# Last feed-forward stage of a two-layer gated cross-attention kernel: four PSUM banks for the down products instead of two, two of them shared with the up products

## The reference

```python
def _L1_ffn_ref(x, W_exp, b_exp, up_weights, up_bias, down_weights, W_con, b_con, down_bias):
    h = jnp.einsum('bsd,dh->bsh', x, W_exp) + b_exp
    h = butterfly(h, up_weights, D_HIDDEN)
    h = jax.nn.gelu(h + up_bias, approximate=False)
    h = butterfly(h, down_weights, D_HIDDEN)
    y = jnp.einsum('bsh,hd->bsd', h, W_con) + b_con
    return y + down_bias
...
x = x + jnp.tanh(g_ffn[1]) * _L1_ffn_ref(_layernorm(x, axis=-1), ...)
```

## Time and profile before

| | |
|---|---|
| runs of the kernel, us | 1150.83, 1146.01, 1144.23; median 1146.01 |
| the profiled execution, us | 1144.74, its span in the profile 1142.9 |
| busy over the span | PE 988.4 us, PEld 866.0, DVE 792.9, ACT 626.3, POOL 235.4 |
| the last stage | from about 943 us to the end of the span |
| slots 0 to 5 | about 25 us each |
| granted TensorE clock, mean | 0.926 of full speed |

### The profile page before, as it was taken

One profiled execution on the slowest core, in us unless ns is written; L12 is line 12 of the kernel. 1 busy time (PEld: TensorE's weight loads), 2 busy tenths in 40 slices (PEclk: granted clock), 3 DMA queues, 4 the chain that ended last, 5 costly groups with the idle time before them and its releaser, 6 DMA issues. The chain is left out here.

```text
span 1142.9 us, 20586 instructions
## 1 busy us (share of the span) xinstructions
PE 988.4 (86%) x6833; PEld 866.0 (76%) x6833; DVE 792.9 (69%) x1588; ACT 626.3 (55%) x1088; POOL 235.4 (21%) x424
## 2 busy tenths in 40 slices
PE   6489999998659998925699994999999989999998
PEld 5367767776448876725588994899999977888888
DVE  5357888875338989979959843677777768656672
ACT  4156666665357779968838543565656544222230
POOL 4213333220129300000002302122111104111210
PEclk9799999999759999967689996999999998999999
DMA  6745554445042237768712366655556610000001
GB/s 197 218 111 138 136 119 124 127 118 173 1 159 111 111 100 241 257 249 306 282 45 91 124 227 162 162 121 118 118 127 127 128 47 1 19 19 31 25 19 38
DMA packets 102808, 143.60 MB, mean 126 GB/s; under 512 B 42951, under 2 KB 76743, under 8 KB 100439
## 3 DMA queue, kind: packets, MB, share of 16 engines
q1 hardware_dynamic: 102438, 141.67, 43.1%
q0 software_dynamic: 304, 1.10, 0.3%
HBM read 76.30 MB, written 47.13 MB: 108 GB/s over the span
## 5 line engine op out<-in xcount | busy, mean ns | idle before, releaser
L41 PE MATMUL bank<-f_xt_hi,f_w_hi 128*128 128x512 f32 x320 | 130.5, 408 | 11.1 <-DMA f_xt_lo<-x_spill 7.9
L42 PE MATMUL bank<-f_xt_lo,f_w_hi 128*128 128x512 f32 x320 | 127.4, 398 | 0.0
L43 PE MATMUL bank<-f_xt_hi,f_w_lo 128*128 128x512 f32 x320 | 127.3, 398 | 0.0
L2631 ACT ACTIVATE f_h<-bank,f_b 128x512 f32<-128x512 f32 x64 | 43.4, 690 | 121.8 <-PE bank L43 74.0
L595 ACT ACTIVATE a_prob<-bank 77x512 f32<-77x512 f32 x128 | 72.5, 591 | 31.5 <-PE bank L759 31.0
L661 DVE TENSOR_REDUCE a_maxima<-bank 128x4 f32<-128x308 f32 x128 | 60.4, 472 | 41.4 <-PE bank L734 41.1
L41 PEld LDWEIGHTS bank<-f_xt_hi,f_w_hi 128*128 128x128 f32 x320 | 61.8, 193 | 27.0 <-DMA f_xt_lo<-x_spill 9.9
L41 PE MATMUL bank<-f_w_hi,f_h_hi 128*128 128x256 f32 x256 | 72.6, 284 | 8.1 <-DVE xres L2596 8.1
L756 PE MATMUL bank<-a_stack,a_kb 96*77 96x256 f32 x256 | 70.8, 299 | 4.7 <-ACT a_mt L588 4.7
L43 PE MATMUL bank<-f_w_hi,f_h_lo 128*128 128x256 f32 x256 | 72.2, 282 | 0.0
L42 PE MATMUL bank<-f_w_lo,f_h_hi 128*128 128x256 f32 x256 | 72.2, 282 | 0.0
(11 more groups left out here) (317 smaller groups left out, 3077.3 us busy)
## 6 DMA issues: line engine op xcount, KB each, us to landing
u_spill<-f_ubuf SPq DMA_DIRECT2D x48, 256.0 KB, 2.5
f_uback<-u_spill SPq DMA_DIRECT2D x24, 512.0 KB, 5.5
a_stack<-a_queries SPq DMA_DIRECT2D x16, 512.0 KB, 4.8
a_q_max<-a_q_hi SPq DMA_DIRECT2D x32, 256.0 KB, 4.9
a_kb<-a_key_spill SPq DMA_DIRECT2D x96, 77.0 KB, 2.5
f_mats<-in_low_steps SPq DMA_DIRECT2D x12, 512.0 KB, 6.6
xres<-in_x SPq DMA_DIRECT2D x16, 256.0 KB, 4.4
a_queries<-a_q_hi SPq DMA_DIRECT2D x16, 256.0 KB, 2.6
```

The source lines that it names most:

```text
L41: nc.tensor.matmul(out, w_hi, m_hi, start=start, stop=False)
L42: nc.tensor.matmul(out, w_hi, m_lo, start=False, stop=False)
L43: return nc.tensor.matmul(out, w_lo, m_hi, start=False, stop=stop)
L2631: act.activation(h[:, n % 2, :], hbank[n % 4][:, :], ACT.Gelu, bias=b1[:, n:n + 1]).then_inc(h_ready, 1)
```

## The change

The four down products of a group get a bank each. y(g, 0) and y(g, 1) stay in O0 and O1; y(g, 2) and y(g, 3) go into `hbank[2]` and `hbank[3]`, which in each slot are free between the up products of tile 6 and 7 of group g + 1 and those of tile 2 and 3 of group g + 2. The waits of PE follow: y(g, 0) and y(g, 1) wait for the sums of the same tiles of the group before, y(g, 2) and y(g, 3) for ACT's gelu of tile 6 and 7 of group g + 1, and h(g, 2) and h(g, 3) from g = 2 on for DVE's sums of tile 2 and 3 of group g - 2. In the last group each down product waits for the sum before it in its bank as well. Nothing is computed differently and no other step moves.

```diff
-        ybank = [O0, O1]
+        ybank = [O0, O1, hbank[2], hbank[3]]
...
-                    dve.scalar_tensor_tensor(out=x, in0=ybank[n % 2][:, 0:D], scalar=tg[:, 0:1], in1=x,
+                    dve.scalar_tensor_tensor(out=x, in0=ybank[n][:, 0:D], scalar=tg[:, 0:1], in1=x,
                                              op0=ALU.mult, op1=ALU.add).then_inc(y_added, 1)
...
                     if n == 0:
                         pe.wait_ge(xt_split, (g + 1) * DC)
-                    if not (isinstance(g, int) and g == 0 and n < 4):
+                    if n in (2, 3) and not (isinstance(g, int) and g < 2):
+
+                        pe.wait_ge(y_added, g * GTT + n - 3 - GTT)
+                    elif not (isinstance(g, int) and g == 0 and n < 4):
                         pe.wait_ge(h_ready, g * HT + n - 3)
...
                     if n == 0:
                         pe.wait_ge(h_split, (g + 1) * HT)
-                    if not (isinstance(g, int) and g == 0 and n < 2):
-                        pe.wait_ge(y_added, g * GTT + n - 1)
+                    if n >= 2:
+                        last_h = min(g + 2, G) if isinstance(g, int) else g + 2
+                        pe.wait_ge(h_ready, last_h * HT + n - 3)
+                    if n < 2 and not (isinstance(g, int) and g == 0) or isinstance(g, int) and g == G - 1:
+
+                        pe.wait_ge(y_added, g * GTT + n + 1 - GTT)
                     for m in range(HT):
-                        last = three_passes(nc, ybank[n % 2][:, 0:D], h_hi[:, par, m, n * P:(n + 1) * P],
+                        last = three_passes(nc, ybank[n][:, 0:D], h_hi[:, par, m, n * P:(n + 1) * P],
```

## The result

| | before | after |
|---|---|---|
| median of the runs, us | 1147.68 (8 runs, 1144.23 to 1157.27) | 1135.30 (8 runs, 1131.01 to 1140.52) |
| ratio after to before | | 0.9888, 95% interval 0.9858 to 0.9917 |
| the profiled execution, us (span) | 1144.74 (1142.9) | 1136.05 (1134.3) |
| first up product of the stage to the last sum, us | 191.91 | 182.18 |

The changed kernel is faster by 1.1%, between 0.8 and 1.4. The forecast was 1136.4; the measured median is 1135.3.

A forecast was written before the change was run, and what follows sets the result against it. PE was taken to bound the last stage, its idle time being y2's wait for DVE's sum. Six slots of 1.60 us give 9.6; 1146.0 - 9.6 = 1136.4 us. Range: from 1134.6 less 1.1 for scatter up to 1141.5.

The forecast's parts named there:

- The removed wait: PE's y2 no longer waits for DVE's sum of y0: 1.60 us a slot, 9.6 us over six slots.
- The added waits: y2, y3 wait for gelus, next slot's h2, h3 for sums: cost 0, with 2.1, 4.3, 4.9, 3.4 us to spare.
- The bound of 1.2 us for satisfied waits: Refill of 0.10 us for each y2 and y3 in six slots; taken as 0, kept for the range.
- What comes next: After the change the next slot moves forward with h0, slots take 23.4 us, nothing in the loop nearer its limit than PE.
- The first rival: y2 stops for gelu 6, or PE meets new waits next slot; half the stall stays, 4.8 us saved, 1141.2; chance 0.12.
- The clock: Loop slots stay at 1.00, no term; rival: up products fall to 0.50, 9.6 us a slot, kernel slower; chance 0.04.
- the sign "less than 9 in the last eight slices": Profile's clock row: such a reading, but for the very end, would show the forecast wrong.
- The median: Whole kernel: median of three runs, 1146.0 us, less 9.6 gives 1136.4.

The follow-up runs named there:

- e3: The changed kernel with its four banks, but y2 again waits for the sum of y0; ratio to before 1.0007, stage 192.84 us.
- e1: The kernel before with only y2 given a bank of its own (hbank[2]), y3 staying in O1; ratio to before 0.9921, stage 182.42 us.
- e2: The kernel before with only y3 given a bank of its own (hbank[3]), y2 staying in O0; ratio to before 0.9983, stage 192.01 us.
- e4: The kernel before, two banks, with DVE's sum of y0 moved ahead of the split of h6; ratio to before 0.9927, stage 182.34 us.
- e7: The changed kernel with y2 in hbank[1] and y3 in hbank[0]; ratio to before 0.9944, stage 188.11 us.
- e6: The changed kernel with 1.4 us of added DVE work ahead of the sum of y0 in slots 0 to 5; ratio to before 0.9896, stage 181.25 us.
- e5: The kernel before with 1.4 us of added DVE work ahead of the sum of y0 in slots 0 to 5; ratio 1.0117, stage 207.58 us.
- e11: The kernel before with 0.7 us of added DVE work ahead of the sum of y0 in slots 0 to 5; ratio 1.0101, stage 201.06 us.
- e8: The changed kernel with the last group written out tile by tile; ratio to before 0.9883, stage 182.38 us.

## Why the prediction was right

**The removed wait.** Forecast 1.60 us in each of six slots, 9.6 in all; the stage is 9.73 shorter, the six slots alone 9.69, and slots take 23.4 us. e3 shows that this one wait carries all of it, e1 and e2 that it is the wait of y2 and not that of y3, e4 that DVE's lateness and not the number of banks is behind it.

**The added waits.** Forecast at zero, with 2.1, 4.3, 4.9 and 3.4 us to spare; measured 2.1 at y2, 4.3 at y3, 4.8 and 3.3 at h2 and h3. e7 shows what the same kind of wait costs where there is no slack. The bound of 1.2 us for satisfied waits was not needed: the seam from y1 to y2 has none.

**What comes next.** DVE is idle for 1.30 us ahead of the sum of y2, where I had 1.0. e6 shows that 1.4 us more work on DVE in every slot costs nothing now. The first rival, a new wait in place of the old, is excluded for this slot length.

**The clock.** It stayed at 1.00 in the slots, and that the denser PE would not make it fall was right. The Trainium skill, TensorE: Matmul & The Clock Gate, section "A second HAM failure mode: psum-queue depth-cycling", would have had it go back and forth; the windows of the slots show 1.00 in both kernels. Two readings in the prediction were off, without weight for the time. A slot has fourteen changes of bank, not six: eight up products, four down products and two transposes, each in another bank than the one before. And the sign "less than 9 in the last eight slices" could not tell anything: the second of these slices shows an 8 in both kernels, since the stage starts there at 0.50. What I had not seen is how near the kernel before was to a fall of the clock: its idle times, not the round of banks, were the danger (e5, e11).

**The median.** 12.4 us less were measured and 9.6 forecast, with an interval of the ratio that corresponds to 9.5 to 16.3 us. The profile gives 9.7 in the stage that was changed, and e1 and e4, whose stage is as short, have ratios of 0.9921 and 0.9927, 8 to 9 us. The remainder beyond 9.7 is most likely scatter of the earlier stages: in fourteen profiles of kernels that do not differ there, the last stage begins between 939.9 and 953.9 us. That the two medians, 1136.4 and 1135.3, lie only 1.1 us apart is in part luck: the forecast started from a median of 1146.0 of three runs, which eight runs put at 1147.7, and the measured gain of the medians is 2.8 us above the forecast one. The two differences go against each other.

## What to carry to other kernels

A wait for a bank turns the lateness of the engine that empties it into idle time of the engine that fills it, so look at where that emptying step stands in its own engine's list: moving it (e4) or handing over a bank that is free just then (the change) brought the same 9.6 to 9.7 us, and the bank gives more slack. When a bank is shared between two products, choose the partner whose next use is furthest away; the change against e7 is 0 against 5.9 us. Price a stall with the clock behind it: here 0.7 us more idle time cost 1.5 us on top in each slot in which TensorE fell to 1.2 GHz.

## What the runs showed of the hardware that was not expected

- Idle times of about 1.5 us on PEld (1.3 on PE) in a stream of matmuls left the granted clock at 1.00 in all six slots; 2.3 us (2.1 on PE) were followed by 0.50 in four of six, 2.9 us (2.7 on PE) in five of six, for 13 to 27 matmuls with 256 columns each at 0.213 us. The fall came at once or up to twelve matmuls later.
- The pace of the down products depends on where their stationary tiles lie in SBUF: in the last slots 0.1167 us a matmul with `f_h_hi` and `f_h_lo` moved by 96 bytes, 0.1200 moved by 128, 0.1200 unmoved. Unmoved, the loop's slots run at 0.1186, now and then one at 0.120. The cause was not found.
- The start of the last stage varies by 14 us between profiles with the same earlier stages, more than the change is worth; the distance inside the stage lies between 182.18 and 182.42 us in the four kernels that lay out and order the stage's PE work alike (after, e1, e4, e8).
